# Thirteen steps of the final stream laid beside the last layer's feed-forward

## The chip, the cores and the metric

One core of a Trainium2 chip. The time is that of one execution in device microseconds (us), the median of several runs.

## The reference

A small language-model tower over B = 2 sequences of T = 1024 tokens, all in float32. Two layers (L = 2, width D = 192, 12 heads, feed-forward 768) of banded attention with one global token; each layer ends in

```python
x = layernorm(x + attention(x) @ Wo.T + bo) * g1 + beta1
x = layernorm(x + relu(x @ W1.T + b1) @ W2.T + b2) * g2 + beta2
```

Then a final layernorm and a projection to 128 channels (Wc) give h. A second block takes h through layernorm, a retention scan and a 5-tap depthwise convolution, and a 128-256-128 gelu feed-forward, each with a residual. A last layernorm feeds a router that sends every token to the best of 8 experts (128-512-128, relu); the expert's result, times the router's probability, is added.

## The kernel before

Tokens lie in blocks of P = 128: NB = 8 per sequence, NN = 16 in all. The five engines run their own queues of instructions in program order; semaphores tie them. The work comes in four rounds (2 sequences x 2 layers), then one stream over the 16 blocks, then the experts. All that the change touches is the last round (`rnd == B * L - 1`, sequence 1, layer 1) and the stream.

**The end of a round.** `_seq_c()` (L1696) writes out by hand the order in which every engine walks the feed-forward; `seq_c(rnd)` (L1724) adapts it, and each engine loops over it (POOL L603, ACT L790, DVE L1069, PE L1554) and picks the kinds that it has a part in:
- `y i`, i below 8: attention's output projection of a block. `y i`, 8 to 15: the second feed-forward product of block i - 8, 12 matmul instructions (L1369). Both go to bank i % 4; PE waits with `z_ready` for z i-4. DVE adds the residual (L1084) and takes mean and variance (L922 to L924); POOL raises the variance to the power -0.5 (L545, `rstd`).
- `z i`: DVE normalizes into `zt` (L928); POOL applies gain and bias into `resid` (L551, L552).
- `tr i`: PE transposes `zt` into bank 4 or 5 (L1304, L1305), ACT writes it to `xa`, `xb` (`norm_out`, L699), the input of hid.
- `hid i`, 0 to 11: six products with W1 for each half of the sequence (four blocks), four matmul instructions of 512 columns each into bank 6 or 7 (L1575, L1576); ACT applies relu (L811).

The order is: y 0 to y 7 with z and tr, hid 0 to 2, tr 4, 5, hid 3 to 5, tr 6, 7, then y 8, y 9, z 8, y 10, z 9, y 11, z 10, z 11, hid 6 to 11, and y 12, y 13, z 12, y 14, z 13, y 15, z 14, z 15. In the last round the tr of 8 and above are left out. At y 9 ACT issues two writes of zero rows to the DRAM table `xs` (L804).

**The stream.** `for t in range(NN + DEPTH)`, 29 steps on each engine (POOL L624, ACT L819, DVE L1141, PE L1593). A block passes a stage per step, so step t has block t at the first stage and block t - 12 near the last:
- DVE, step t: adds of blocks t-7 and t-11 from PSUM (L1147, L1152), statistics of four kinds (L1157 to L1175) on block t, t-7, t-11, t-3, the scan of block t-5 (L1185), and, after POOL's power of the step before (L637), the normalizations z0 of block t-1, z1 and x of t-4, z2 of t-8 and the router's row of t-12 (all L1193).
- PE: the convolution of block t-6, ten matmul instructions (L1601), transposes of z0 (L1607, L1608), the scan's product (L1612), the second and first gelu products of t-10 and t-9 (m2 L1619, m1 L1627), the transpose of z1 (L1634), the router's product of t-13 (L1641); then hw, the projection to 128 channels of block t-1 (L1650, L1651), and the transposes of z2 (L1656) and of the router's row (L1661).
- ACT: moves the transposes out of PSUM (L824, L825 into `xa`, `xb`; L837 xn; L842 h0, counted by `kept`; L846; L851) and does gelu (L831). An activation of the 1 x 1 `gs` (L818) ahead of the stream loads Gelu's table.
- POOL: adds (L628, L629, L634) and the power of -0.5 (L637).
In steps 17, 22, 26 and 28 (`CHOSEN`) the router's choice is made for a group of blocks, and POOL scatters rows to `xs` (L619). Experts start when all rows are there.

SP waits for the last y product and then loads the experts' weights. In SBUF the tensors from `h0` on share the space of the attention's; with the declared order only the experts' weights lie ahead of the stream's small buffers.

Of the kernel before, what the change touches and what calls it, by code (L numbers as in the profile page):

```python
# [16 lines left out]
P = 128  # L17
# [10 lines left out]
KC = 5  # L28
# [48 lines left out]
ORDER = (1, 2, 3, 0, 4, 5, 6, 7)  # L77
CHOSEN = tuple(e - 1 + DEPTH for _, e in GROUPS)
# [12 lines left out]
def program(nc, x, xcol, pad, emb, wqkv, wo, w1, w2, lnr, lnl, lnf, wc, ident, band, cols, decay, convw, wout, bo2, owner,  # L91
            ln12, aw1, ab1, aw2, ab2, wg, bg, mwb, mw2, mb2, route, earlier, qrows, krows, out):
    with ExitStack() as ctx:
# [128 lines left out]
        rs = sb("rs", [P, 2, 5], F32)  # L222
        xt = sb("xt", [P, XBUF, RW], F32)
# [191 lines left out]

        def early_step(j, part):

            return -LEAD + PARTS * (j - 3) + part if j >= 3 else None
# [106 lines left out]
        def _(pool):  # L525
# [21 lines left out]

            def residual(b, j):
# [61 lines left out]
            pool.wait_ge(const_in, 16 * len(consts))  # L610
            nc.gpsimd.tensor_tensor(bo2b[:, 0, :], bo2b[:, 0, :], bo2b[:, 1, :], ALU.add).then_inc(bo2_ready, 1)
            pool.wait_ge(bo2_ready, 1)
# [11 lines left out]
            for t in range(NN + DEPTH):  # L624
                i = t - 5
                if 0 <= i < NN:
                    pool.wait_ge(x1_ready, i + 1)
                    nc.gpsimd.tensor_tensor(h0[:, i, :], h0[:, i, :], ab2b[:, :], ALU.add)  # L628
                    nc.gpsimd.tensor_tensor(x1[:, i, :], x1[:, i, :], bo2b[:, 0, :], ALU.add).then_inc(xb_ready, 1)  # L629
                i = t - 8  # L630
                if 0 <= i < NN:
                    pool.wait_ge(xb_ready, i + 1)
                    pool.wait_ge(y_added, i + 1)
                    nc.gpsimd.tensor_tensor(h0[:, i, :], h0[:, i, :], x1[:, i, :], ALU.add).then_inc(xh_ready, 1)  # L634
                if t < NN + DEPTH - 2:
                    pool.wait_ge(stats_ready, t + 1)
                    nc.gpsimd.tensor_tensor(rs[:, t % 2, :], vin[:, t % 2, :], colc[:, 3:4].to_broadcast([P, 5]),  # L637
                                            ALU.pow).then_inc(rs_ready, 1)
# [23 lines left out]
        def _(act):  # L662
# [14 lines left out]
            def first_pieces(j, q):  # L677

                act.wait_ge(qk_mm, at(qk_mm, j + 1, q))
                if j >= 2:  # L680
# [3 lines left out]
                                     ACT.Copy).then_inc(qk_hi, 1)  # L684

# [16 lines left out]
            for b in range(B):  # L702
                for l in range(L):
# [86 lines left out]
                    for kind, i in seq_c(rnd):  # L790
# [15 lines left out]
                        if kind == "hid":  # L806
# [4 lines left out]
                            nc.scalar.activation(hid[:, m, :], ps[6 + i % 2][:, :], ACT.Relu).then_inc(h_relu, 1)  # L811
                            if rnd == 0 and i == FF // P:
# [5 lines left out]
            nc.scalar.activation(gs[0:1, 0, 0:1], lfa[0:1, 0:1], ACT.Gelu)  # L818
            for t in range(NN + DEPTH):  # L819
                i = t - 1  # L820
                if 0 <= i < NN:
                    n = i % NB
                    act.wait_ge(t0_mm, i + 1)
                    nc.scalar.activation(xa[:, blk(n)], ps[0][0:DLO, 0:P], ACT.Identity, bias=lfa[:, 1:2], scale=lfa[:, 0:1])  # L824
                    nc.scalar.activation(xb[0:DHI, blk(n)], ps[0][0:DHI, P:2 * P], ACT.Identity, bias=lfb[0:DHI, 1:2],  # L825
                                         scale=lfb[0:DHI, 0:1]).then_inc(a0_done, 1)
                i = t - 9
                if 0 <= i < NN:
                    act.wait_ge(m1_mm, i + 1)
                    for m in range(2):  # L830
                        ins = nc.scalar.activation(gl[:, i % 2, m, :], ps[7][:, blk(m)], ACT.Gelu, bias=ab1s[:, m:m + 1])  # L831
                    ins.then_inc(gelu_done, 1)
                i = t - 4
                if 0 <= i < NN:
                    b, n = divmod(i, NB)
                    act.wait_ge(t1_mm, i + 1)
                    nc.scalar.activation(xn[:, b, 2 + n * P:2 + (n + 1) * P], ps[1][:, 0:P], ACT.Identity, bias=l12[:, 1:2],  # L837
                                         scale=l12[:, 0:1]).then_inc(a1_done, 1)
                i = t - 1
                if 0 <= i < NN:  # L840
                    act.wait_ge(hw_mm, i + 1)
                    nc.scalar.activation(h0[:, i, :], ps[6][:, 0:DM], ACT.Copy).then_inc(kept, 1)  # L842
                i = t - 8
                if 0 <= i < NN:
                    act.wait_ge(t2_mm, i + 1)
# [975 lines left out]
```

## Time and profile before

| | |
|---|---|
| median of 3 runs | 919.44 us (919.04 to 920.62) |
| profiled execution, its own time | 919.02 us |
| its span, first to last instruction | 916.9 us |
| mean granted TensorE clock | 0.953 |
| PE, DVE, ACT, POOL busy | 809.2, 634.4, 563.3, 567.2 us |
| last feed-forward, hid 0 to the end of y 15 | 715.6 to 754.6 |
| stream, DVE's step 0 to its step 28 | 757 to about 848 |
| experts | about 863 to the end |

The granted clock is given as a share of 2.4 GHz: 1.00 is that, 0.50 is 1.2 GHz. PE is TensorE's matmuls, PEld its weight loads. A timeline's row gives start, length, engine, line, operation, output <- input, count, and in brackets the idle time before it and what ended it.

### The profile page before, as it was taken

The numbers are of one execution on the slowest core, as the hardware profiler recorded it, in microseconds if no ns is written. First come the engines' busy times: TensorE is split into PE (matmuls) and PEld (weight loads), VectorE is DVE, ScalarE is ACT, GpSimd is POOL, SyncE is SP. The second block draws the span as 40 slices with busy tenths as digits, with TensorE's granted clock in tenths as the row PEclk, the third lists the DMA queues.
The fourth block names the chain that finished last, engine by engine and source line by source line (L and its number), as shares of the span: only waits on it lengthen the run. The fifth ranks groups of instructions, "written<-read, shape, count | busy, mean of one in ns | idle before, by whom it ended". The sixth has DMA issues, their size and how long they took to land.

```text
span 916.9 us, 23665 instructions
## 1 busy us (share of the span) xinstructions
PE 809.2 (88%) x8467; PEld 617.3 (67%) x8467; DVE 634.4 (69%) x1959; ACT 563.3 (61%) x1559; POOL 567.2 (62%) x820
## 2 busy tenths in 40 slices
PE   5979998999999989989999899999998986887397
PEld 2757766576777666667776666677766664876397
DVE  2769975547899655578997553689975436988454
ACT  2858885437788853267888543778885423565164
POOL 3638885545388856475888554438885546759345
PEclk8989998999999999999999999999999996997599
DMA  2310000142000012430000024200000245001331
GB/s 65 105 47 3 4 13 11 58 139 77 6 4 3 13 35 87 114 92 26 3 3 14 11 81 116 79 5 4 3 3 2 79 121 205 1 3 41 93 103 39
DMA packets 38595, 43.84 MB, mean 48 GB/s; under 512 B 7162, under 2 KB 33881, under 8 KB 38345
## 3 DMA queue, kind: packets, MB, share of 16 engines
q1 hardware_dynamic: 18348, 19.40, 7.1%
q10 hardware_dynamic: 17860, 18.19, 6.7%
q0 software_dynamic: 2272, 4.74, 1.7%
q8 instruction: 69, 1.13, 0.5%
q14 instruction: 46, 0.38, 0.1%
HBM read 20.70 MB, written 21.59 MB: 46 GB/s over the span
## 4 chain that ended last, share of the span: by engine, by line
PE 59%; DVE 21%; issue 5%; SPq 4%; POOL 4%; ACT 4%; DMA 3%; POOLq 0%; DVEq 0%; ACTq 0%
PE bank L1369 7%; DVE p L1011 6%; DVE nmx L1002 5%; PE bank L1575 5%; PE bank L1457 5%; PE bank L1576 5%; PE bank L1506 4%; PE bank L1530 4%; PE bank L1395 3%; PE bank L1406 3%; PE bank L1460 2%; PE bank L1509 2%; PE bank L1680 2%; PE bank L1601 2%; PE bank L1689 2%
## 5 line engine op out<-in xcount | busy, mean ns | idle before, releaser
L573 POOL TENSOR_TENSOR p<-p 128x384 f16<-128x384 f32 (+1 forms) x320 | 283.8, 907 | 103.4 <-ACT p L746 98.7
L1002 DVE TENSOR_REDUCE nmx<-bank 128x1 f32<-128x384 f32 (+1 forms) x384 | 190.6, 511 | 20.7 <-PE bank L1460 16.2
L744 ACT ACTIVATE p<-bank 128x384 f32<-128x384 f32 (+1 forms) x384 | 170.9, 452 | 54.3 <-PE bank L1509 38.0
L1506 PE MATMUL bank<-stack 103*128 103x128 bf16 x1056 | 145.1, 222 | 5.6 <-DMA stack<-mtr 5.1
L746 ACT ACTIVATE p<-bank 128x384 f16<-128x384 f32 (+1 forms) x320 | 144.3, 451 | 0.0
L1509 PE MATMUL bank<-bandb,idb 128*128 128x128 bf16 x672 | 135.3, 222 | 0.0
L1530 PE MATMUL bank<-vst,p 128*128 128x49 bf16 x2112 | 115.8, 185 | 15.2 <-DVE p L1011 13.6
L1457 PE MATMUL bank<-stack 100*128 100x384 bf16 (+1 forms) x384 | 121.2, 316 | 7.3 <-DVE nmx L1002 2.9
L1530 PEld LDWEIGHTS bank<-vst,p 128*128 128x128 f16 x2112 | 89.5, 97 | 32.4 <-DVE p L1011 19.1
L1506 PEld LDWEIGHTS bank<-stack 103*128 103x128 bf16 x1056 | 88.3, 98 | 29.7 <-issue 14.5
L1460 PE MATMUL bank<-bandb,idb 128*128 128x128 bf16 x672 | 101.2, 220 | 0.0
L545 POOL TENSOR_TENSOR rstd<-ve,colc 128x1 f32<-128x1 f32 x64 | 35.2, 550 | 101.7 <-DVE ve L924 101.7
L1084 DVE TENSOR_TENSOR bank<-bank,resid 128x192 f32<-128x192 f32 x64 | 23.1, 361 | 82.8 <-PE bank L1369 82.8
L1460 PEld LDWEIGHTS bank<-bandb,idb 128*128 128x128 bf16 x672 | 66.0, 98 | 20.9 <-issue 0.8
L811 ACT ACTIVATE hid<-bank 128x512 f32<-128x512 f32 x48 | 28.7, 597 | 81.8 <-PE bank L1576 81.8
L758 ACT ACTIVATE stack<-bank 96x1024 bf16<-96x1024 bf16 x64 | 65.1, 1017 | 18.6 <-PE bank L1395 17.2
L1395 PE MATMUL bank<-idb,hid 128*96 128x128 bf16 x768 | 59.3, 221 | 10.1 <-POOL hid L590 5.2
L1369 PE MATMUL bank<-w2s,hid 128*128 128x192 f32 x384 | 65.1, 328 | 2.8 <-ACT hid L811 2.8
L1369 PEld LDWEIGHTS bank<-w2s,hid 128*128 128x128 f32 x384 | 62.3, 190 | 7.2 <-issue 7.2
L1395 PEld LDWEIGHTS bank<-idb,hid 128*96 128x96 bf16 x768 | 51.2, 124 | 23.4 <-issue 16.8
L1509 PEld LDWEIGHTS bank<-bandb,idb 128*128 128x128 bf16 x672 | 65.6, 98 | 0.7
L1011 DVE TENSOR_TENSOR p<-p 128x384 f16<-128x384 f32 (+1 forms) x64 | 63.2, 987 | 2.2
(253 smaller groups left out, 1818.0 us busy)
## 6 DMA issues: line engine op xcount, KB each, us to landing
xs<-zrow ACTq DMA_DIRECT2D x8, 2193.0 KB, 13.5
xt<-xs SPq DMA_DIRECT2D x23, 129.0 KB, 2.1
w2s<-in_w SPq DMA_DIRECT2D x4, 576.0 KB
mwbs<-in_mwb SPq DMA_DIRECT2D x1, 2064.0 KB, 8.5
mw2s<-in_mw SPq DMA_DIRECT2D x1, 2048.0 KB, 12.8
lnrow<-in_lnr SPq DMA_DIRECT2D x4, 480.0 KB
stack<-mtr SPq DMA_DIRECT2D x96, 3.0 KB
w1b<-in_w SPq DMA_DIRECT2D x4, 291.0 KB
```

The lines of the kernel that those rows point to most:

```text
L573: nc.gpsimd.tensor_tensor(p2[:, u % RING, 0:w], p32[:, u % RING, 0:w], p1[:, u % RING, 0:w], ALU.subtract).then_inc(p2_pool, 1)
L744: ins = nc.scalar.activation(p32[:, s % RING, 0:w], ps[2 + s % 3][:, 0:w], ACT.Exp)
L746: ins = nc.scalar.activation(p1[:, s % RING, 0:w], ps[2 + s % 3][:, 0:w], ACT.Exp)
L1002: nc.vector.tensor_reduce(nmx[:, vn % 3, h:h + 1], nat_bank(v)[:, 0:w], AX.X, ALU.max, negate=True).then_inc(max_done, 1)
L1011: nc.vector.tensor_tensor(p2[:, u % RING, 0:w], p32[:, u % RING, 0:w], p1[:, u % RING, 0:w], ALU.subtract).then_inc(p2_dve, 1)
L1369: ins = mm(y, hid[:, m, blk(n % BPC)], w2s[:, m, :], start=m == 0, stop=m == FF // P - 1)
L1395: ins = nc.tensor.transpose(psb[3 + (3 * b + g) % 2][0:NPIECE, blk(h)], nat[:, b % 2, g * HG + h, :], idb[:, :])
L1457: mm(s_ps[:, 0:len(win) * P], q, stack[0:K_NAT, H + h, blk(win[0], len(win))], start=True, stop=False)
L1460: ins = mm(s_ps[:, blk(i)], idb[:, :], bandb[:, 0 if m < n else 1, :], start=False, stop=(i, m) == edges[-1])
L1506: ins = mm(ps[2 + s % 3][:, blk(i)], stack[0:K_ALL, H + h, blk(m)], stack[0:K_ALL, h, blk(n)], start=True, stop=m == n)
L1509: ins = mm(ps[2 + s % 3][:, blk(i)], idb[:, :], bandb[:, 1 if m < n else 0, :], start=False, stop=True)
L1530: ins = mm(out_ps, pt[:, w % RING, blk(a)], vst[:, m, h, :], start=False, stop=i == HH - 1 and a == len(win) - 1 and pt is p2)
```

## The change

The loop bodies of the stream become functions of t: `stream(t)` on DVE and POOL, `stream_head(t)` and `stream_rest(t)` on PE and ACT. In the last round `seq_c` calls steps 0 to 12 from within the feed-forward; the loops after it start at 13.

```diff
+FILLED = 13
...
+STREAM = {("hid", 1): 1, ("hid", 2): 2, ("hid", 3): 3, ("hid", 4): 4, ("hid", 5): 5, ("hid", 6): 6, ("hid", 7): 7,
+          ("hid", 8): 8, ("hid", 9): 9, ("hid", 10): 10, ("hid", 11): 11}
 def seq_c(rnd):
+    if rnd == B * L - 1:
+        seq = []
+        for kind, i in _seq_c():
+            if kind == "tr" and i >= NB:
+                continue
+            t = STREAM.get((kind, i))
+            if t is not None:
+                seq += [("stat", t), ("head", t), (kind, i), ("rest", t)]
+                continue
+            if (kind, i) == ("hid", 0):
+                seq.append(("stat", 0))
+            if (kind, i) == ("y", 15):
+                seq.append(("stat", 12))
+            seq.append((kind, i))
+            if (kind, i) == ("y", 15):
+                seq += [("head", 12), ("rest", 12)]
+        return seq
```

`stat` is DVE's and POOL's part, `head` and `rest` are PE's and ACT's. On PE `head` holds the convolution, the z0 transposes, scan's product, m2, m1, the z1 transpose and the router's product; `rest` holds hw and the transposes of z2 and of the router's row. On ACT `head` holds the two moves of z0, gelu and xn, `rest` the moves to h0, ht and xm. On every engine a part is issued whole at its place in the order.

The y products of the last round rotate through other banks, so that 0 to 3 are free for the stream:

```diff
+        def y_bank(i, last):
+            return ps[(6 if i >= NB + BPC else 4) + i % 2 if last and i >= NB else i % 4][:, 0:D]
...
             def y_block(i):
                 n = block_of(i)
-                if i >= 4:
-                    pe.wait_ge(z_ready, at(z_ready, i - 3))
-                y = ps[i % 4][:, 0:D]
+                last = rnd == B * L - 1
+                if last and i in (NB, NB + 1):
+                    pe.wait_ge(ln_out, at(ln_out, i - 1))
+                elif i >= 4:
+                    pe.wait_ge(z_ready, at(z_ready, i - 1 if last and i >= NB else i - 3))
+                y = y_bank(i, last)
```

The stream's banks change with it: convolution and scan's product from 4 to 3, m2 from 3 to 5, m1 from 7 to 4, hw from 6 to 2, the router's product from 5 to 6, its ranks from 2 to 7. The first use of each such bank in the stream waits for the z that frees it, for example

```diff
             def stream_head(t):
                 i = t - 6
                 if 0 <= i < NN:
                     b, n = divmod(i, NB)
                     pe.wait_ge(a1_done, min(i + 2, (b + 1) * NB))
                     if i:
                         pe.wait_ge(y_added, i)
+                    else:
+                        pe.wait_ge(z_ready, START[z_ready.num][B * L - 1] + NB)
```

hid still reads `xa` and `xb`, so z0's transposes go to `ata` and `atb`, which the last round no longer needs. The call that loads Gelu's table, and the set-up of DVE and POOL, stand in step 0 of the functions:

```diff
+            def stream_head(t):
+                if t == 0:
+                    nc.scalar.activation(gs[0:1, 0, 0:1], lfa[0:1, 0:1], ACT.Gelu)
                 i = t - 1
                 if 0 <= i < NN:
                     act.wait_ge(t0_mm, i + 1)
-                    nc.scalar.activation(xa[:, blk(n)], ps[0][0:DLO, 0:P], ACT.Identity, bias=lfa[:, 1:2], scale=lfa[:, 0:1])
+                    nc.scalar.activation(ata[:, blk(i % NB)], ps[0][0:DLO, 0:P], ACT.Identity, bias=lfa[:, 1:2],
+                                         scale=lfa[:, 0:1])
...
-            for t in range(NN + DEPTH):
+            for t in range(FILLED, NN + DEPTH):
+                stream_head(t)
+                stream_rest(t)
```

In SBUF the stream's small buffers (`z0` to `rs`) are declared ahead of the experts' weights, so that they lie in space that the attention's `stack` no longer needs.

## Rows read from the trace of the kernel before

**Rows 1.** Busy by stretch: length; PE, PEld, DVE, ACT, POOL; clock; DMA; GB/s.

```profile
735.50:746.50 11.00, 10.28 (x24) 4.16 (x22) 1.98 (x6) 3.65 (x7) 3.81 (x7) 1.00 0.68 193
...
761.00:773.80 12.80, 8.77 (x32) 6.48 (x33) 8.64 (x50) 5.80 (x16) 8.18 (x10) 0.50 0.65 244
773.80:799.20 25.40, 22.43 (x169) 20.22 (x168) 21.28 (x109) 13.75 (x42) 16.61 (x27) 0.94 0.00 1
```

**Rows 2.** Timeline of TensorE, last feed-forward; a bracket holds the idle time before.

```profile
715.62 1.12 PE L1575 MATMUL bank<-xa,w1a 96*128 96x512 f32 x2 [0.24 <-ACT xb L699]
...
727.42 8.04 PE L1369 MATMUL bank<-w2s,hid 128*128 128x192 f32 x48 [0.34 <-ACT hid L811]
...
746.56 8.04 PE L1369 MATMUL bank<-w2s,hid 128*128 128x192 f32 x48 [0.78 <-ACT hid L811]
761.00 0.45 PE L1607 MATMUL bank<-idf,z 128*96 128x128 f32 x1 [6.41 <-DVE z L1193]
```

**Rows 3.** Timeline of DVE, y 9 to z 11 of that feed-forward.

```profile
731.60 0.37 DVE L1084 TENSOR_TENSOR bank<-bank,resid 128x192 f32<-128x192 f32 x1 [0.78 <-PE bank L1369]
...
732.73 0.48 DVE L928 TENSOR_SCALAR zt<-bank,mv,rstd 128x192 f32<-128x192 f32 x1
...
737.43 0.48 DVE L928 TENSOR_SCALAR zt<-bank,mv,rstd 128x192 f32<-128x192 f32 x1 [0.33 <-POOL rstd L545]
```

**Rows 4.** Timeline of POOL: last residuals, and powers of steps 0, 1.

```profile
722.34 0.59 POOL L552 TENSOR_TENSOR resid<-resid,lnrow 128x192 f32<-128x192 f32 x1
...
758.28 0.59 POOL L552 TENSOR_TENSOR resid<-resid,lnrow 128x192 f32<-128x192 f32 x1
...
759.35 2.32 POOL L637 TENSOR_TENSOR rs<-vin,colc 128x5 f32<-128x5 f32 x2
```

**Rows 5.** Timeline of TensorE in step 10, to the start of step 11.

```profile
787.63 1.38 PE L1601 MATMUL bank<-diag,xn 128*128 128x128 f32 x10
788.85 0.27 PE L1607 MATMUL bank<-idf,z 128*96 128x128 f32 x1
...
789.29 0.61 PE L1619 MATMUL bank<-aw2s,gl 128*128 128x128 f32 x4
789.74 0.61 PE L1627 MATMUL bank<-ht,aw1s 128*128 128x128 f32 x4
...
790.29 0.39 PE L1650 MATMUL bank<-wca,xa 96*128 96x128 f32 x2
...
790.74 0.27 PE L1656 MATMUL bank<-idf,z 128*128 128x128 f32 x1
791.41 1.38 PE L1601 MATMUL bank<-diag,xn 128*128 128x128 f32 x10 [0.40 <-ACT xn L837]
```

**Rows 6.** Timeline of DVE: step 6's start and z0; starts of steps 12, 13.

```profile
771.63 0.35 DVE L1157 BATCH_NORM_STATS2 sums<-resid 128x6 f32<-128x192 f32 x1
...
773.54 0.35 DVE L1193 TENSOR_SCALAR z<-resid,mean,rs 128x192 f32<-128x192 f32 x1
...
793.27 0.29 DVE L1147 TENSOR_TENSOR x<-bank,x 128x128 f32<-128x128 f32 x1
...
797.13 0.28 DVE L1147 TENSOR_TENSOR x<-bank,x 128x128 f32<-128x128 f32 x1
```

**Rows 7.** Timeline of ACT: tr 6's first part, and the Gelu table.

```profile
727.17 0.45 ACT L699 ACTIVATE xa<-bank,lna 96x128 f32<-96x128 f32 x1
...
746.43 1.28 ACT L818 ACT_TABLE_LOAD   x1
747.73 0.20 ACT L818 ACTIVATE gs<-lfa 1x1 f32<-1x1 f32 x1
```

**Rows 8.** Busy time by stretch, around a short gap of TensorE.

```profile
576.10:577.70 1.60, 0.01 (x1) 0.02 (x1) 1.53 (x5) 0.85 (x3) 1.60 (x5) 1.00 0.22 47
...
578.60:582.30 3.70, 3.70 (x22) 3.00 (x21) 1.85 (x5) 2.74 (x5) 0.64 (x2) 0.54 0.25 86
```

**Rows 9.** Timeline of POOL, the first scatter.

```profile
826.72 1.09 POOL L619 DMA_INDIRECT xs<-trow,slot  x1
```

More of the change, by code:

```diff
@@ L684, in first_pieces, with stream_rest @@
                                      ACT.Copy).then_inc(qk_hi, 1)
+            def stream_head(t):
+                if t == 0:
+                    nc.scalar.activation(gs[0:1, 0, 0:1], lfa[0:1, 0:1], ACT.Gelu)
+                i = t - 1
+                if 0 <= i < NN:
+                    act.wait_ge(t0_mm, i + 1)
+                    nc.scalar.activation(ata[:, blk(i % NB)], ps[0][0:DLO, 0:P], ACT.Identity, bias=lfa[:, 1:2],
+                                         scale=lfa[:, 0:1])
+                    nc.scalar.activation(atb[0:DHI, blk(i % NB)], ps[0][0:DHI, P:2 * P], ACT.Identity, bias=lfb[0:DHI, 1:2],
+                                         scale=lfb[0:DHI, 0:1]).then_inc(a0_done, 1)
+                i = t - 9
+                if 0 <= i < NN:
+                    act.wait_ge(m1_mm, i + 1)
+                    for m in range(2):
+                        ins = nc.scalar.activation(gl[:, i % 2, m, :], ps[4][:, blk(m)], ACT.Gelu, bias=ab1s[:, m:m + 1])
+                    ins.then_inc(gelu_done, 1)
+                i = t - 4
+                if 0 <= i < NN:
+                    b, n = divmod(i, NB)
+                    act.wait_ge(t1_mm, i + 1)
+                    nc.scalar.activation(xn[:, b, 2 + n * P:2 + (n + 1) * P], ps[1][:, 0:P], ACT.Identity, bias=l12[:, 1:2],
+                                         scale=l12[:, 0:1]).then_inc(a1_done, 1)
+            def stream_rest(t):
+                i = t - 1
+                if 0 <= i < NN:
+                    act.wait_ge(hw_mm, i + 1)
+                    nc.scalar.activation(h0[:, i, :], ps[2][:, 0:DM], ACT.Copy).then_inc(kept, 1)
+                i = t - 8
+                if 0 <= i < NN:
+                    act.wait_ge(t2_mm, i + 1)
+                    nc.scalar.activation(ht[:, i % 2, :], ps[0][:, 0:P], ACT.Identity, bias=l12[:, 3:4],
+                                         scale=l12[:, 2:3]).then_inc(a2_done, 1)
+                i = t - 12
+                if 0 <= i < NN:
+                    act.wait_ge(t3_mm, i + 1)
+                    nc.scalar.activation(xm[:, i % 2, :], ps[1][:, 0:P], ACT.Copy).then_inc(a3_done, 1)
             for k in range(2 * NC):
@@ L811, in _ @@
                             nc.scalar.activation(hid[:, m, :], ps[6 + i % 2][:, :], ACT.Relu).then_inc(h_relu, 1)
+                        if kind == "head":
+                            stream_head(i)
+                        if kind == "rest":
+                            stream_rest(i)
+                        if kind == "hid":
                             if rnd == 0 and i == FF // P:
@@ L1216, in _ @@
+            for t in range(FILLED, NN + DEPTH):
+                stream(t)
                 if t in CHOSEN:
@@ new lines, in stream_rest @@
+            def stream_rest(t):
+                i = t - 1
+                if 0 <= i < NN:
+                    pe.wait_ge(a0_done, i + 1)
+                    if i:
+                        pe.wait_ge(kept, i)
+                    else:
+                        pe.wait_ge(z_ready, START[z_ready.num][B * L - 1] + NB - 1)
+                    mm(ps[2][:, 0:DM], ata[:, blk(i % NB)], wca[:, :], start=True, stop=False)
+                    mm(ps[2][:, 0:DM], atb[0:DHI + 1, blk(i % NB)], wcb[0:DHI + 1, :], start=False, stop=True).then_inc(hw_mm, 1)
+                i = t - 8
+                if 0 <= i < NN:
+                    pe.wait_ge(z2_ready, i + 1)
+                    pe.wait_ge(a0_done, min(t, NN))
+                    nc.tensor.transpose(ps[0][:, 0:P], z2[:, i % 2, :], idf[:, :]).then_inc(t2_mm, 1)
+                i = t - 12
+                if 0 <= i < NN:
+                    pe.wait_ge(z3_ready, i + 1)
+                    pe.wait_ge(a1_done, min(t - 3, NN))
+                    nc.tensor.transpose(ps[1][:, 0:P], trow[:, i, 0:DM], idf[:, :]).then_inc(t3_mm, 1)
@@ L1568, in _ @@
                             ln_transpose(i, i, D)
+                        if kind == "head":
+                            stream_head(i)
+                        if kind == "rest":
+                            stream_rest(i)
                         if kind == "hid":
@@ L1662, in _ @@
+            for t in range(FILLED, NN + DEPTH):
+                stream_head(t)
+                stream_rest(t)
                 if t in CHOSEN:
```

385 lines of the change are left out of this document (175 added, 210 removed).

## The prediction

> **What bounds the kernel now.** I read four views in this order: the busy time by stretch, TensorE's timeline in the last feed-forward, the other engines' timelines beside it, and the clock around a short gap. By stretch [rows 1], TensorE is slow just where the final stream starts: 8.77 of 12.8 us busy at a granted clock of 0.50 (1.2 GHz) in 761.0 to 773.8, behind a gap of 6.41 us [rows 2], then 22.43 of 25.4 us busy up to 799.2. So steps 0 to 5 of the stream leave TensorE room, and steps 6 to 12 nearly none. In the feed-forward it is the other way round: TensorE runs its hid and y products without a pause [rows 2] and DVE is 1.98 us busy in 11 [rows 1]. The change lays the one over the other. What can be gained is the gap and the half rate up to 773.8; what is paid is TensorE work that now stands between the hid products, and waits.
>
> The time is measured from marks in the profiled execution (919.02 us; its span is 916.9 and the rest lies around it; the median of the runs is 0.4 above it). The mark I follow is the start of DVE's step 13, 797.13 us [rows 6], since what follows it is the same in both kernels. Ahead of the mark the stream and the feed-forward take 715.62 to 797.13; I lay out the same stretch for the new order.
>
> **First half, hid 0 to 5 with steps 0 to 5.** hid 0 starts at 715.62 and a hid product takes 1.72 (two pairs of 0.86), so hid 1 stood at 717.34. Now the transposes of step 1 stand ahead of it, in order. They need z0, that needs the power of step 0 on POOL, and POOL first ends the residual of z 7 at 722.34 + 0.59 = 722.93 [rows 4]. In the kernel before the power starts 0.48 after the last residual (758.87 to 759.35), and TensorE's transpose starts 1.65 after that (761.00) [rows 2, 4]. The same spacing gives 725.06: TensorE stands still for 7.7 us. Each of steps 1 to 3 then adds its transposes, 0.22, and the hw product, 0.45 [rows 5] (0.44 stands there for the transposes and the scan's product together, 0.45 for hw); steps 4 and 5 add another transpose, 0.11. Together 3.5. y 8 waits for ACT's second pair of norm_out, which stands behind relu and kept of step 5: two ACTs of 0.45 [rows 7], of which some 0.5 was waited for before too, +0.3.
> The clock: the gap of 7.6 us is longer than the 6.41 us behind which it stood at 0.50 [rows 1, 2]. After a gap of 1.60 us dense work ran on, and of it 3.7 us at a mean clock of 0.54 [rows 8], 1.85 lost; I take 2.0 here, for a clock already down when work resumes. Sum of the half: 7.7 + 3.5 + 0.3 + 2.0 = +13.5.
>
> **The y products.** Before they rotate through four banks; now y 10 waits for z 8, y 11 for z 9, and in the second half y 14 for z 12, y 15 for z 13. On DVE, z 8 is queued behind the adding and the statistics of y 9: 731.60 for y 9's add, 732.73 for z 8, end 733.21 [rows 3]. The y block starts at 727.42 and a product takes 1.95 (8.04 for four, less the tail) [rows 2], so y 10 stood at 731.3 and now starts at 733.3. Then DVE takes y 10's add and statistics ahead of z 9, and y 11 waits 1.9 again. Behind these waits on TensorE stands everything that follows. +3.9 for the four, and +3.9 for y 12 to 15.
>
> **Second half, hid 6 to 11 with steps 6 to 11.** The convolution of step 6 can follow y 11 at once. The transpose of z0 cannot: DVE has z 11 first (it starts at 737.43 and takes 0.48, 2.45 in all from the end of the y products at 735.46 [rows 2, 3]), then step 6 of the stream, whose z0 starts 1.91 into the step and takes 0.35 [rows 6]. TensorE goes on 4.6 after y 11's end, of which 1.2 is convolution. From there it is the bound, and I add its work, each operation by the distance of the starts in step 10 [rows 5]: convolution 1.22 (1.11 to 1.22 in other steps), transposes and scan product 0.44, m2 0.45, m1 and t1 0.55, hw 0.45, t2 0.11, and 1.72 for hid. Step 6 from the transpose on 2.7; step 7 3.9; step 8 4.0; step 9 (with m1) 4.4; steps 10 and 11 (with m2) 4.95 each: 24.9. DVE's step of 3.86 at the most [rows 6] is covered by these, as are ACT's and POOL's parts; if that cover failed, the third rival below comes true. The preload of Gelu's table is called for step 0 of ACT's head alone, and the new order has no such call, so the load (1.28 [rows 7]) falls in step 9, between the transposes and the normalized xn that the next convolution wants; some 2.3 us of hid and hw cover most of the 2.6, +0.3. With 0.1 for the last relu: 4.6 + 24.9 + 0.4 = 29.9 from y 11's end to y 12, against 746.56 - 735.46 = 11.1 before [rows 2]: +18.8.
> The Trainium skill (ScalarE: Activation LUTs, What ACT_TABLE_LOAD costs) gives a drain of about 1.38 us beside the load; the trace has none (the activation starts 1.30 after the load begins), and by the page the sum would be 1.4 higher.
>
> **The end.** y 12 then stands at 746.56 + 13.5 + 3.9 + 18.8 = 782.8, y 15 9.8 later at 792.6. DVE takes step 12 (3.86) ahead of y 15, then y 15's add up to z 15, which like y 11's up to z 11 takes 1.93 and 0.48 (two spacings of 1.95 behind 731.60 the add of y 11 stood at 735.50 [rows 3]): step 13 starts at 792.6 + 6.2 = 798.8, against 797.13. **+1.7**, if the clock falls once only.
> The other drops: TensorE is idle 1.9 ahead of y 10, 1.9 ahead of y 11, 3.4 in step 6, and 1.9 ahead of y 14 and y 15. The row that is nearest is the gap of 1.6 us with 3.7 us at about half rate behind it. No row shows such gaps with bursts of 2 us between them. The bounds for the first group are 0 and 5.8 (y 10 and y 11 wholly at half rate, 1.95 each, and 1.85 at hid 6); I take y 11 and hid 6, 3.8. For the second 0 and 3.9; y 15 at half rate is hidden by DVE's step 12, so part of y 14, 1.0. Below zero neither can go, as the waits are there at either rate. Sum: 1.7 + 3.8 + 1.0 = +6.5, so 919.0 + 6.5, and 0.4 more as median: 925.9.
>
> **Costed at nothing.** The two writes of zero rows, issued at y 9, are over in the stretch up to 746.5 (a DMA share of 0.68 [rows 1]); they move some 17 us later. SP's loads of expert weights wait for the last y product; they are over in the stretch up to 773.8 (0.65 [rows 1]) and move some 40 later. The first scatter that needs the one is at 826.72 [rows 9], and the experts come behind it. The exchange of xa, xb for ata, atb, the other banks and the SBUF order change no duration. POOL's adds and powers of the moved steps fit its idle: 3.81 us busy in 11 at 735.5 to 746.5 [rows 1].
>
> **Rivals.** *The clock holds after the first gap* (y 10 to 15 at full rate): +1.7, 921.1, no measurable change. For it: bursts and hid products are dense once running. Against: the 1.6 us gap [rows 8]. Chance 0.15. The Trainium skill (TensorE: Matmul & The Clock Gate, HAM oscillation) says that a loop whose bursts are shorter than the waits between them pays the slow clock at each; no row here shows that pattern yet.
> *The y products keep their pace*, because z 8, z 9, z 12 and z 13 come in time: this needs each z done within 1.9 us of its own y product, where its place behind the next add puts it 3.8 after. Then 7.8 and the later drops go: 1.7 - 7.8 = -6.1, 913.3, faster. Against it stands the order in DVE's queue, which I can read; but every other gain that I overlook (shorter waits at step 1 or step 6) ends here too. Chance 0.15.
> *Each mixed step waits for a handshake besides its work*, as TensorE waited 0.40 before step 11 for xn [rows 5], now with relu in ACT's queue too: 0.6 in each of 11 steps is 6.6, 932.5. Decides from the point where ACT's or DVE's chain is longer than TensorE's step. Chance 0.17.
> Forecast 0.53.
>
> **Numbers.** A measurement can tell about 0.2%, 1.8 us, from no change. Faster takes the second rival and some of the first: 0.18. Same takes the rest of the first, 0.12, and 0.02 of the forecast's low end: 0.14. Slower 0.68. The range reaches from near the second rival, 914.5, to past the third, 933.5.
>
> **What would show it.** TensorE waits some 7.7 us for z0 ahead of hid 1; y 10, y 11, y 14 and y 15 each start 1.9 us after the product ahead of them has ended; the granted clock falls again in the y block of the first half; the spacing of hid 9, 10, 11 is 4.4 to 5.0 us; DVE's step 13 starts near 803.5. It is wrong if the y products follow each other at 1.95, if the spacing in steps 6 to 11 is over 5.5 us, or if the mark comes ahead of 797.

## The result, and the profile after

The changed kernel takes 923.96 us (median of 6 runs, 919.23 to 926.20), the kernel before 919.24 on the same chip (6 runs, 915.40 to 920.62): a ratio of 1.006, 95% interval 1.0038 to 1.0082. It is slower, by some 4.7 us. The ratios are taken over the single executions, not from the two medians, and of the 25 runs of the kernel before that stand beside e5 to e8 further down, one took 2581.37 us and is left out of the ratios.

| | before | after |
|---|---|---|
| profiled execution, its span | 919.02, 916.9 us | 919.23, 917.0 us |
| mean granted TensorE clock | 0.953 | 0.960 |
| PE, DVE, ACT, POOL busy | 809.2, 634.4, 563.3, 567.2 us | 805.4, 635.3, 561.9, 568.0 us |
| last feed-forward, hid 0 to the end of y 15 | 715.6 to 754.6 | 711.5 to 794.1 |
| DVE's step 13 | 797.13 | 798.02 |

The two profiled executions are equally long though the medians are not. So the first thing to see is where the profiled run of after was ahead. Its hid 0 stands at 711.45 us, that of before at 715.62 [rows 2], in code that is the same up to there. The busy time by stretch of both, over two stretches of that code (length; busy time of PE, PEld, DVE, ACT, POOL with instructions in brackets; granted clock; DMA; GB/s), the kernel before first:

```profile
60.00:70.00 10.00, 8.01 (x80) 6.04 (x80) 5.41 (x12) 6.30 (x23) 5.05 (x9) 0.66 0.01 2
...
570.00:590.00 20.00, 18.00 (x132) 13.49 (x131) 12.49 (x38) 13.73 (x30) 11.26 (x26) 0.91 0.22 60
```

And the kernel after:

```profile
60.00:70.00 10.00, 7.65 (x86) 5.79 (x87) 6.21 (x13) 6.54 (x24) 5.83 (x10) 0.83 0.01 2
...
570.00:590.00 20.00, 18.00 (x153) 13.22 (x152) 14.13 (x40) 15.80 (x33) 10.48 (x25) 1.00 0.30 86
```

Where the clock falls in the earlier rounds differs from run to run; the profiled run of after had the higher clock in both stretches (0.83 for 0.66, 1.00 for 0.91) and is the fastest of its six. Over all that stands ahead of hid 0 TensorE lost 13.0 us to a low clock in it and 15.8 in the run of before (busy time times 1 minus the granted clock, in stretches of 0.5 us): 2.7 of the 4.2 us. The rest was not taken apart. From here on every time is counted from the start of hid 0 of its own run; the stretch from there to DVE's step 22 is nearly all that the kernels differ in.

TensorE at the start of the last feed-forward, kernel after (start, length, line, operation, count, idle time before it and what ended it):

```profile
711.45 1.13 PE L1693 MATMUL bank<-xa,w1a 96*128 96x512 f32 x2 [0.24 <-ACT xb L747]
712.42 1.02 PE L1694 MATMUL bank<-xb,w1b 97*128 97x512 f32 x2
720.89 0.45 PE L1421 MATMUL bank<-idf,z 128*96 128x128 f32 x1 [7.45 <-DVE z L1010]
...
721.34 1.92 PE L1693 MATMUL bank<-xa,w1a 96*128 96x512 f32 x2
```

The gap of 6.41 us that stood at the start of the stream [rows 2] is not gone. It stands ahead of hid 1 and measures 7.45. On DVE step 0's statistics follow z 7, and on POOL step 0's power follows the last residual of z 7 (DVE's first row is step 0, POOL's rows are that residual and the powers of steps 0 and 1):

```profile
717.11 0.36 DVE L974 BATCH_NORM_STATS2 sums<-resid 128x6 f32<-128x192 f32 x1
718.16 0.59 POOL L577 TENSOR_TENSOR resid<-resid,lnrow 128x192 f32<-128x192 f32 x1
...
719.23 2.32 POOL L570 TENSOR_TENSOR rs<-vin,colc 128x5 f32<-128x5 f32 x2
```

The half rate [rows 1] came along, as the stretches show:

```profile
717.50:721.00 3.50, 0.11 (x1) 0.12 (x2) 2.18 (x15) 0.00 (x0) 3.34 (x6) 0.50 0.01 2
721.00:727.50 6.50, 6.50 (x14) 3.62 (x15) 2.53 (x18) 2.47 (x6) 2.07 (x3) 0.50 0.00 0
...
738.50:750.50 12.00, 8.60 (x50) 8.01 (x51) 4.07 (x14) 0.62 (x2) 3.94 (x7) 1.00 1.04 322
750.50:754.50 4.00, 1.10 (x10) 0.91 (x9) 3.48 (x16) 0.00 (x0) 2.57 (x5) 1.00 0.52 157
754.50:758.50 4.00, 3.39 (x8) 2.10 (x9) 3.56 (x17) 1.15 (x3) 3.82 (x7) 0.57 0.00 0
758.50:782.00 23.50, 23.23 (x145) 17.62 (x143) 13.05 (x65) 14.32 (x38) 10.83 (x17) 1.00 0.00 1
782.00:794.00 12.00, 8.53 (x50) 7.97 (x51) 6.23 (x27) 0.44 (x2) 4.75 (x10) 1.00 0.01 1
```

6.50 us of hid products ran wholly at 0.50 (1.2 GHz). The y block takes 12.0 us, 8.6 of them busy, where it was one unbroken row of 8.04 before [rows 2]; the last row but one shows TensorE busy for 23.23 of 23.5 us, the bound that the prediction gave it. The y products themselves and step 6 behind them:

```profile
738.48 4.17 PE L1400 MATMUL bank<-w2s,hid 128*128 128x192 f32 x24 [0.67 <-ACT xb L747]
744.35 2.22 PE L1400 MATMUL bank<-w2s,hid 128*128 128x192 f32 x12 [1.70 <-DVE zt L950]
748.26 2.22 PE L1400 MATMUL bank<-w2s,hid 128*128 128x192 f32 x12 [1.70 <-DVE zt L950]
750.32 1.28 PE L1413 MATMUL bank<-diag,xn 128*128 128x128 f32 x10
755.11 0.45 PE L1421 MATMUL bank<-idf,z 128*96 128x128 f32 x1 [3.51 <-DVE z L1010]
```

y 8 and y 9 run as one row, y 10 and y 11 each wait 1.70 us for a z. (The profile's rows overlap a little: the starts of y 10 and y 11 are 3.91 apart instead of 1.95, so a wait costs 1.96.) DVE's own timeline shows the ring: the add of y 9, z 8 behind it, and only then y 10's add after 2.31 idle:

```profile
742.69 0.37 DVE L1187 TENSOR_TENSOR bank<-bank,resid 128x192 f32<-128x192 f32 x1 [0.78 <-PE bank L1400]
...
743.82 0.48 DVE L950 TENSOR_SCALAR zt<-bank,mv,rstd 128x192 f32<-128x192 f32 x1
746.60 0.37 DVE L1187 TENSOR_TENSOR bank<-bank,resid 128x192 f32<-128x192 f32 x1 [2.31 <-PE bank L1400]
```

In the second half y 14 and y 15 do the same, again TensorE's timeline of after:

```profile
787.91 2.22 PE L1400 MATMUL bank<-w2s,hid 128*128 128x192 f32 x12 [1.70 <-DVE zt L950]
791.83 2.22 PE L1400 MATMUL bank<-w2s,hid 128*128 128x192 f32 x12 [1.70 <-DVE zt L950]
```

And DVE's timeline there: step 12 stands ahead of y 15's add, and step 13 follows at 798.02:

```profile
791.69 0.28 DVE L964 TENSOR_TENSOR x<-bank,x 128x128 f32<-128x128 f32 x1
...
795.62 0.35 DVE L1187 TENSOR_TENSOR bank<-bank,resid 128x192 f32<-128x192 f32 x1
...
798.02 0.28 DVE L964 TENSOR_TENSOR x<-bank,x 128x128 f32<-128x128 f32 x1
```

Where the 5 us come from, by the same marks in both traces (us):

| stretch | before | after | difference |
|---|---|---|---|
| hid 0 to y 8; before with the part of the stream up to step 6, after with steps 0 to 5 inside | 26.38 | 27.03 | +0.65 |
| y 8 to the end of y 11 | 7.88 | 11.84 | +3.96 |
| second half up to y 12, with steps 6 to 11 | 32.90 | 31.76 | -1.14 |
| y 12 to step 13 | 14.36 | 15.94 | +1.58 |
| sum, hid 0 to step 13 | 81.52 | 86.57 | +5.05 |

Laying steps 0 to 11 over the hid products gained half a microsecond in all, with what the low clock costs in either kernel; the two stretches that hold the y products' waits cost 5.5.

### The profile page after: what moved, and what is told of

It reads as the page before. It is cut to its first block, busy times and chain, and to the rows that moved or that the text cites. A ratio compares the mean times of both kernels' runs of the same rounds, so it can differ in the third digit from the quotient of the medians.

```text
span 917.0 us, 23670 instructions
## 1 busy us (share of the span) xinstructions
PE 805.4 (88%) x8467; PEld 614.5 (67%) x8467; DVE 635.3 (69%) x1959; ACT 561.9 (61%) x1558; POOL 568.0 (62%) x820
## 3 DMA queue, kind: packets, MB, share of 16 engines
q8 instruction: 69, 1.13, 0.5%
## 4 chain that ended last, share of the span: by engine, by line
PE 58%; DVE 22%; POOL 5%; issue 5%; SPq 4%; ACT 3%; DMA 2%; POOLq 0%; DVEq 0%; ACTq 0%
PE bank L1400 7%; DVE p L1114 6%; PE bank L1571 5%; DVE nmx L1105 5%; PE bank L1693 5%; PE bank L1694 4%; PE bank L1620 4%; PE bank L1644 4%; PE bank L1509 3%; PE bank L1520 3%; PE bank L1574 2%; PE bank L1623 2%; PE bank L1732 2%; PE bank L1741 2%; SPq L462 2%
```

## The experiments

The table holds every kernel that ran. The marks are us behind the run's own hid 0. "Lost" is TensorE's time lost to a low clock within 104 us of hid 0: busy time times (1 - granted clock), summed over stretches of 0.5 us. The marks and the loss come from one profiled run of each. The ratio is to the kernel before on the same chip; e1 to e4 ran together (before: median 921.84 of 35 runs), e5 to e8 together on another chip (before: 918.91 of 25).

| kernel | y 8 | y 12 | step 13 | step 22 | lost | median us | ratio, 95% interval |
|---|---|---|---|---|---|---|---|
| before | 11.80 | 30.94 | 81.51 | 116.32 | 5.93 | | |
| after | 27.03 | 70.63 | 86.57 | 121.50 | 5.02 | 923.96 | 1.006, 1.0038 to 1.0082 |
| e1_banks | 26.83 | 66.58 | 80.56 | 116.61 | 6.59 | 920.57 | 0.9988, 0.9967 to 1.001 |
| e2_warm | 23.75 | 65.77 | 81.73 | 117.92 | 1.55 | 922.10 | 0.9998, 0.9977 to 1.002 |
| e3_late | 21.15 | 62.30 | 86.77 | 121.91 | 7.84 | 923.52 | 1.003, 1.0005 to 1.0055 |
| e4_second | 12.40 | 47.05 | 82.14 | 116.98 | 3.42 | 920.98 | 0.9988, 0.9964 to 1.0012 |
| e5_second_banks | 12.41 | 43.79 | 77.95 | 112.79 | 5.71 | 913.19 | 0.9951, 0.9929 to 0.9973 |
| e6_banks_warm | 23.76 | 61.46 | 75.44 | 110.73 | 0 | 910.68 | 0.9929, 0.9903 to 0.9956 |
| e7_second_warm | 12.67 | 41.71 | 72.86 | 107.70 | 0 | 908.90 | 0.991, 0.9877 to 0.9942 |
| e8_before_warm | 11.80 | 30.94 | 77.13 | 111.94 | 0 | 912.84 | 0.9952, 0.993 to 0.9973 |

For most kernels the difference at step 22 and the ratio tell the same: +5.2 against 0.6% (5.5 us) for after, -4.4 against -0.48% for e8, -8.6 against -0.9% for e7. They are up to 2.8 us apart for others: +5.6 against 0.3% for e3, +1.6 against nothing for e2. So differences of 1 to 2 us between two kernels at that mark hang on single runs.

**e1_banks: the y products' waits taken away.** The waits hang on the banks that the y products may use, so the experiment gives them others, and moves the waits to where nothing is lost.

```diff
-            return ps[(6 if i >= NB + BPC else 4) + i % 2 if last and i >= NB else i % 4][:, 0:D]
+            return ps[{8: 4, 9: 5, 10: 6, 11: 7, 12: 6, 13: 7, 14: 2, 15: 6}[i] if last and i >= NB else i % 4][:, 0:D]
...
+                elif last and i == 14:
+                    pe.wait_ge(kept, 11)
+                elif last and i == 15:
+                    pe.wait_ge(z_ready, at(z_ready, 13))
                 elif i >= 4:
-                    pe.wait_ge(z_ready, at(z_ready, i - 1 if last and i >= NB else i - 3))
+                    pe.wait_ge(z_ready, at(z_ready, i - 3))
...
+                    if t == 12:
+                        pe.wait_ge(z_ready, START[z_ready.num][B * L - 1] + 15)
...
+                            if rnd == B * L - 1 and i in (6, 7):
+                                pe.wait_ge(z_ready, at(z_ready, i + 5))
```

> The y products of the last round get other banks: y 10 and y 11 take 6 and 7 (hid 6 and hid 7 then wait for z 10, z 11), y 14 takes 2, y 15 takes 6 and waits only for z 12. Nothing else is changed. Theory of the bank waits: TensorE's three waits on the path go, 1.9 us each ahead of y 10, y 11 and y 14 (the one ahead of y 15 is hidden by DVE's step 12), so 5.6 us less than the changed kernel: 924.0 to 918.4. Rival, the waits are hidden by something else (DVE's z 11 and step 6 come at the same time anyway): no change, 924. Rival of the clock: the shorter stretch leaves the drops at steps 1 and 6 as they are, so it adds or takes nothing.

Measured: 0.9988, and 4.9 less than after at step 22. TensorE's timeline of this kernel:

```profile
740.64 8.07 PE L1404 MATMUL bank<-w2s,hid 128*128 128x192 f32 x48 [0.67 <-ACT xb L747]
748.54 1.28 PE L1417 MATMUL bank<-diag,xn 128*128 128x128 f32 x10
753.33 0.33 PE L1425 MATMUL bank<-idf,z 128*96 128x128 f32 x1 [3.52 <-DVE z L1010]
```

The block is one row of 8.07 again. From after's y 8 to its y 12 it saves 3.85, by step 13 6.0; 1.1 of that goes again by step 22, where the clock fell once more (from 84.0 to 87.5 behind hid 0). The waits are real and cost nearly what they seem to (4.9 of the 5.6 expected); without them the change is worth nothing either way.

**e2_warm: the clock held through the waits.** Products of the identity with itself go to a part of a bank that nobody reads, 32 ahead of step 1's transposes and 14 ahead of step 6's. They only keep TensorE busy while it would wait.

```diff
+                    if t == 6:
+                        pe.wait_ge(z_ready, START[z_ready.num][B * L - 1] + 10)
+                    for _ in range({1: 32, 6: 14}.get(t, 0)):
+                        mm(ps[{6: 7}.get(t, 5)][:, 3 * P:4 * P], idf[:, :], idf[:, :], start=True, stop=True)
```

> TensorE does idle products while it waits for z0: 32 of 128 x 128 ahead of step 1's transposes (some 7.1 us) and 14 ahead of step 6's (3.1 us), into banks that nobody reads; their results are used nowhere. Theory of the clock: the profile of the changed kernel shows 6.6 us and 3.3 us of dense work at 0.50 behind the two waits, 5 us lost; with the waits filled the clock stays at 1.00 there and the time falls by some 5 us, 924.0 to 919.0. Rival, the half rate is hidden behind DVE and POOL (the path runs through z0 and the powers): less than 1 us.

Measured: 0.9998. TensorE's timeline of this kernel:

```profile
717.50 7.31 PE L1419 MATMUL bank<-idf 128*128 128x128 f32 x64
725.13 0.32 PE L1425 MATMUL bank<-idf,z 128*96 128x128 f32 x1 [0.33 <-DVE z L1010]
...
725.39 1.02 PE L1697 MATMUL bank<-xa,w1a 96*128 96x512 f32 x2
```

And its busy time by stretch:

```profile
717.50:725.10 7.60, 7.30 (x65) 7.11 (x63) 4.68 (x27) 0.60 (x1) 7.21 (x13) 1.00 0.01 3
725.10:739.40 14.30, 13.50 (x60) 8.09 (x60) 6.95 (x40) 10.37 (x29) 6.53 (x7) 1.00 0.00 0
```

The transposes start 9.46 behind hid 0, as in after (9.44), so the wait is untouched. What changed is the rate: the pair behind them takes 1.02, where it took 1.92 in after. y 8 comes 3.3 earlier, y 12 4.9 earlier: the two low stretches of after, 3.39 and 1.63. At step 22 3.6 are left, because a new low stretch (1.55 lost) came later in the stream, in step 13. TensorE's wait ahead of it, and the stretch:

```profile
800.72 0.45 PE L1425 MATMUL bank<-idf,z 128*96 128x128 f32 x1 [1.55 <-DVE z L1010]
800.40:803.90 3.50, 3.18 (x16) 3.17 (x17) 2.74 (x12) 1.14 (x4) 2.61 (x5) 0.51 1.09 448
```

By the ratio the gain over after is 0.6%, which is what was expected; by the mark it is 3.6 of the 5 us.

**e3_late: the stream begins at hid 2,** when the residual of z 7 is nearly done, so that no long wait stands ahead of a hid product. Steps 1 to 9 then lie beside hid 3 to 11, step 10 behind y 15.

```diff
-FILLED = 13
+FILLED = 11
...
+STREAM = {("hid", 3): 1, ("hid", 4): 2, ("hid", 5): 3, ("hid", 6): 4, ("hid", 7): 5, ("hid", 8): 6, ("hid", 9): 7, ("hid", 10): 8, ("hid", 11): 9}
```

> The steps start two hid products later: step 0 on DVE and POOL at hid 2, steps 1 to 9 beside hid 3 to 11, step 10 at y 15, so steps 11 and 12 go back to the stream behind. Theory of the wait for z0 in step 1: TensorE reaches it with 5.6 instead of 1.8 us of work behind it, waits 3.8 instead of 7.5 us, and two steps' work leaves each half. First half 7.4 us shorter, second half 6.0, end 0.6, stream two steps longer, 7.8: 6 us less than the changed kernel, 918. Rival, steps are worth moving wherever they stand (each saves its 3.9 us of stream): it gets slower than the changed kernel.

Measured: 1.003, no better than after at step 22 (121.91 against 121.50), so the expectation missed. TensorE's wait for z0 in step 1 is 3.58, as expected, but y 8 came only 5.9 earlier (7.4 expected) and y 8 to y 12 is 2.5 shorter (6.0 expected), y 12 so 8.3 earlier in all. Then steps 11 and 12 are back in the stream, and the clock was low three times (3.3, 2.89 and 1.65 lost). The stretches of the second and the third:

```profile
749.20:756.20 7.00, 5.89 (x15) 3.77 (x16) 4.74 (x20) 2.30 (x6) 4.98 (x8) 0.51 0.01 3
...
793.20:797.20 4.00, 3.44 (x17) 3.43 (x18) 2.99 (x15) 1.40 (x5) 2.79 (x5) 0.57 1.10 456
```

Against after, 7.84 - 5.02 = 2.8 us more were lost to the clock, which is up to that much of the missing gain; the rest was not taken apart.

**e4_second: only the second half is filled.** hid 0 to 4 run without a step between them; step 0 stands at hid 5, steps 1 to 6 beside hid 6 to 11, step 7 behind y 15.

```diff
-FILLED = 13
+FILLED = 8
...
+STREAM = {("hid", 6): 1, ("hid", 7): 2, ("hid", 8): 3, ("hid", 9): 4, ("hid", 10): 5, ("hid", 11): 6}
```

> Nothing beside the first half: step 0 on DVE and POOL at hid 5, steps 1 to 6 beside hid 6 to 11, step 7 at y 15, steps 8 to 12 back in the stream behind. Theory: the first half is as in the kernel before (15.2 us shorter than in the changed one), the second half 11.5 shorter, the end 0.9, and the stream 17.0 longer: 10.6 us less than the changed kernel, 913.4, so 6 us faster than the kernel before. Rival, the loss sits in the second half, where TensorE's own work adds up, and the first half pays: then this is no better than the changed kernel.

Measured: 0.9988, 4.5 better than after at step 22 where 10.6 had been expected. y 8 is 0.6 later than before; a wait for z0 (4.44 us) now stands behind y 11, and the clock falls behind it. From y 12 to step 13 it takes 35.09, and there the clock falls a second time; e7, without bank waits and low clock, takes 31.15 for the same. The stretches of e4:

```profile
741.10:745.50 4.40, 0.04 (x1) 0.00 (x0) 3.82 (x15) 0.00 (x0) 2.91 (x6) 1.00 0.69 184
745.50:750.50 5.00, 4.91 (x14) 2.89 (x15) 1.94 (x12) 2.06 (x6) 2.22 (x2) 0.66 0.00 0
...
783.00:788.00 5.00, 4.97 (x29) 4.87 (x29) 3.97 (x22) 2.71 (x6) 3.93 (x8) 0.66 1.04 440
```

What this wait is made of can be read from the same trace. The first row is POOL's power of step 0, the second DVE's z0 from it, the third TensorE's transpose:

```profile
724.56 1.18 POOL L570 TENSOR_TENSOR rs<-vin,colc 128x5 f32<-128x5 f32 x1
744.75 0.78 DVE L1010 TENSOR_SCALAR z<-resid,mean,rs 128x192 f32<-128x192 f32 x1
745.59 0.32 PE L1421 MATMUL bank<-idf,z 128*96 128x128 f32 x1 [4.44 <-DVE z L1010]
```

The power was there at 725.74, 19 us ahead of z0. DVE computes z0 in its step 1, and that stands behind z 11 in its queue: the wait comes of the order alone.

**e5_second_banks** is e4 with e1's banks (y 14 waits for kept 6, step 7's hw for z 15).

```diff
+                elif last and i == 14:
+                    pe.wait_ge(kept, 6)
...
+                    if t == 7:
+                        pe.wait_ge(z_ready, START[z_ready.num][B * L - 1] + 15)
```

> Steps 1 to 6 beside the second half alone, as in e4_second, with the y banks of e1_banks. Theory of the bank waits: as in e1_banks the waits ahead of y 10, y 11 and y 14 go, 5.6 us less than e4_second, so about 0.994 of its ratio: 0.993 of the kernel before, 913. By marks: DVE's add of step 22, 117.0 us behind hid 0 in e4_second, at 111.4. Rival of the clock: with the waits gone TensorE is no longer idle there, and a drop goes too, up to 2 us more. Rival, the waits were hidden in this order: no change against e4_second.

Measured: 0.9951, 4.2 less than e4 at step 22. The banks are worth about the same in both places, 4.9 on after and 4.2 on e4. The expectation had 5.6 and, in the rival of the clock, one low stretch less; more was lost to the clock instead, 5.71 against 3.42 in e4, as 6.59 against 5.02 in e1. If that was all on the path, the banks gave 6.5 us in both places, an estimate from these four losses and marks.

**e6_banks_warm** is e1 with idle products ahead of steps 1, 6, 12 and 13, and Gelu's table loaded at step 0, early, as the kernel before had it.

```diff
+                        if kind == "stat" and i == 0:
+                            nc.scalar.activation(gs[0:1, 0, 0:1], lfa[0:1, 0:1], ACT.Gelu)
...
+                    if t in {6: 10, 12: 14}:
+                        pe.wait_ge(z_ready, START[z_ready.num][B * L - 1] + {6: 10, 12: 14}[t])
+                    for _ in range({1: 32, 6: 14, 12: 6, 13: 8}.get(t, 0)):
+                        mm(ps[{1: 5, 6: 5, 12: 7, 13: 7}[t]][:, 3 * P:4 * P], idf[:, :], idf[:, :], start=True, stop=True)
```

> All thirteen steps moved, y banks of e1_banks, Gelu's table loaded at step 0 again, and idle products in TensorE's waits: 32 ahead of step 1, 14 ahead of step 6, 6 ahead of step 12's and 8 ahead of step 13's transposes (results used nowhere). The trace of e1_banks has three stretches at 0.50 ahead of step 22, with 6.6 us lost, and step 9 pays 0.4 for the table. Theory, bank waits and clock explain the loss and add up: the add of step 22, 116.6 behind hid 0 in e1_banks, comes at 110, and the time is 0.992 of the kernel before, 912 to 914. Rival, the half rate is hidden behind DVE and POOL: 116.

Measured: 0.9929. At step 22 it is 10.8 ahead of after; e1 and e2 alone were 4.9 and 3.6 ahead. It is the whole change, all 13 steps where the change puts them, with both costs taken out.

**e7_second_warm** is e5 with the same treatment: 18 idle products ahead of step 1, 4 and 8 ahead of steps 7 and 8.

```diff
+                    if t in {1: 10, 7: 14}:
+                        pe.wait_ge(z_ready, START[z_ready.num][B * L - 1] + {1: 10, 7: 14}[t])
+                    for _ in range({1: 18, 7: 4, 8: 8}.get(t, 0)):
+                        mm(ps[{1: 5, 7: 7, 8: 7}[t]][:, 3 * P:4 * P], idf[:, :], idf[:, :], start=True, stop=True)
```

> As e5_second_banks, with Gelu's table loaded at step 0 and idle products ahead of the transposes of step 1 (18), 7 (4) and 8 (8). Theory of the clock: the two stretches at 0.50 of e4_second (1.7 us each) go: 3.4 less than e5_second_banks, the add of step 22 at 108, 0.989 of the kernel before. If it equals e5_second_banks, the clock was not on the path. Against e6_banks_warm it tells whether the first half is worth anything once waits and clock are out: equal says that steps 1 to 5 cost in the first half what they cost in the stream.

Measured: 0.991, 908.9 us, the fastest of all. TensorE's timeline ahead of and at step 1's transposes:

```profile
738.32 4.20 PE L1425 MATMUL bank<-idf 128*128 128x128 f32 x36
742.93 0.31 PE L1431 MATMUL bank<-idf,z 128*96 128x128 f32 x1 [0.41 <-DVE z L1012]
```

And its busy time by stretch from there on, at a clock of 1.00 throughout:

```profile
742.90:759.40 16.50, 16.19 (x75) 10.22 (x75) 9.44 (x52) 9.96 (x27) 9.02 (x10) 1.00 0.07 20
759.40:771.80 12.40, 11.01 (x71) 10.38 (x72) 8.42 (x33) 1.23 (x4) 6.51 (x11) 1.00 0.22 63
771.80:790.60 18.80, 16.82 (x137) 15.48 (x138) 17.28 (x84) 9.17 (x28) 15.11 (x25) 1.00 0.56 211
```

**e8_before_warm** is the kernel before with nothing moved: 28 idle products ahead of step 1's transposes, 3 ahead of each hw of steps 1 to 5.

```diff
+                    for _ in range(28 if t == 1 else 0):
+                        mm(ps[7][:, 3 * P:4 * P], idf[:, :], idf[:, :], start=True, stop=True)
                     pe.wait_ge(z0_ready, i + 1)
...
+                    for _ in range(3 if t <= 5 else 0):
+                        mm(ps[7][:, 3 * P:4 * P], idf[:, :], idf[:, :], start=True, stop=True)
                     pe.wait_ge(a0_done, i + 1)
```

> The kernel before, with nothing moved: 28 idle products ahead of step 1's transposes and 3 ahead of each hw of steps 1 to 5, so that TensorE stays busy in the gap ahead of the stream. The trace before has 17 us at 0.50 there, about 5.9 us of TensorE's time. Theory, half rate on TensorE's chain is what the move saves: the add of step 22 comes 3 to 5 us earlier than 116.3, and the time is 0.995 to 0.997 of the kernel before, with nothing moved. Rival, DVE, ACT and POOL set the pace of steps 0 to 6 whatever the clock: no change.

Measured: 0.9952. The same stretches as in [rows 1], laid 0.8 earlier, as its hid 0 stands at 714.79:

```profile
760.18:773.00 12.82, 10.97 (x81) 9.40 (x82) 10.48 (x59) 7.09 (x20) 9.42 (x12) 1.00 0.64 242
773.00:798.40 25.40, 22.60 (x185) 20.62 (x184) 23.67 (x122) 15.30 (x47) 18.07 (x29) 1.00 0.00 1
```

In [rows 1] the first read 0.50. The clock stays whole and step 13 comes 4.4 earlier; y 8, y 12 and the distance from step 13 to step 22 (34.81) are what they were. The gap stays, filled with idle products; what its half rate costs could be had for less than the change: 4.4 us of the 5.93 lost, with no step moved.

## Why the prediction was right, and where its terms were off

The sign and the range held: forecast 925.9, measured 923.96; by the marks +5.05 where +6.5 was forecast. Term by term, counted from hid 0:

| term | forecast | measured |
|---|---|---|
| idle ahead of hid 1 | 7.7 | 7.45 |
| steps' work in the first half, with y 8's wait | 3.8 | 4.4 (15.23 - 7.45 - 3.39) |
| half rate behind the first wait | 2.0 | 3.39 |
| y 10 and y 11 | 3.9 | 3.96 |
| end of y 11 to y 12, without the clock (forecast from the end of y 11's row, measured from the start of what follows, 0.16 earlier) | 29.9 | 30.13 (31.76 - 1.63) |
| clock behind y 10's wait | 3.8 | 1.63 |
| y 12 to y 15 | 9.8 | 9.75 |
| clock behind y 14's and y 15's waits | 1.0 | 0 |
| y 15 to step 13 | 6.2 | 6.19 |

**What was read from queues held to 0.3 us.** That z 8 stands behind y 9's add on DVE, that step 12 stands ahead of y 15's add, that z0 of step 6 comes behind z 11: each gave its wait (3.96 for 3.9, 6.19 for 6.2, and 7.45 for 7.7 ahead of hid 1). The work of the steps in the first half was put 0.6 too low. e1 confirms by experiment what the y waits are worth: without them the changed kernel is no slower than before. The rival in which the y products keep their pace was rejected for the right reason.

**The step that failed is the clock.** The forecast took 2.0 for the first stretch, "for a clock already down when work resumes", from a stretch [rows 8] behind a gap of 1.60; the nearer row was the gap of 6.41 with 0.50 behind it [rows 1, 2], and what followed 7.45 us was 6.50 us of dense work at half rate. In the other direction it took 4.8 for falls behind y 10 and behind y 14. The clock read 1.00 through both y blocks (738.5 to 750.5, 782.0 to 794.0), waits included, and fell once more, behind the idle 3.51 us of step 6. The three errors, +1.4, -2.2 and -1.0, make -1.8; the other terms bring back 0.4 (from the same starting point the row of 29.9 is off by 0.1 only), and -1.4 is what lies between forecast and marks. That the errors partly cancel is luck. The first rival had said that the clock holds through the y blocks, and was right about that; its 921.1 left out the fall at step 6 and had the first one at 2.0 too. On the oscillation that the Trainium skill describes (TensorE: Matmul & The Clock Gate, HAM oscillation), for bursts shorter than the waits between them, this trace does not decide: the bursts here are 2.22 us and the waits 1.70.

**The third rival,** a handshake in each mixed step, did not come: hid 8 to 11 start 3.83, 4.40, 5.22 and 4.84 us apart, 4.4 to 5.0 had been forecast for the last three, and TensorE is 99% busy there. The 5.22 holds Gelu's table, in step 9 as forecast, since the order never calls step 0 of ACT's head:

```profile
769.59 1.28 ACT L710 ACT_TABLE_LOAD   x1
770.88 0.37 ACT L710 ACTIVATE gl<-bank,ab1s 128x128 f32<-128x128 f32 x1
```

The activation starts 1.29 after the load; the extra drain that the Trainium skill gives (ScalarE: Activation LUTs, What ACT_TABLE_LOAD costs) is not seen here either, so the sum without it was the better one.

**Why the change doesn't pay.** The gap of 6.41 and the half rate were what could be gained. The profile after shows that in the order that the change gives them they were not on offer in the first half. z0 waits for the power of step 0. The power stands in POOL's queue behind the last residual of z 7, which ends 7.3 us behind hid 0 (718.16 + 0.59 - 711.45), and the statistics of step 0 stand behind z 7 on DVE. Taking steps 0 to 5 to hid 1 to 5 puts the wait of the stream's start ahead of hid 1 instead.

That wait is one of order in the queues and not of data. Block 0 of the stream is the first block of sequence 0, whose residual POOL wrote two rounds earlier. In the trace of after it ends at 365.46, 350 us ahead of step 0's statistics, and DVE waits for `resid_ready` with the count of that round:

```profile
364.87 0.59 POOL L577 TENSOR_TENSOR resid<-resid,lnrow 128x192 f32<-128x192 f32 x1
```

The `stack`, in whose space the change puts the stream's small buffers, is read for the last time at 699.4, 12 us ahead of hid 0. POOL is idle for 2.76 us up to 704.38, and a power takes 1.2. The bank that the transposes of step 1 go to is free with z 5, which ends at 713.48, just as hid 0 does (713.44) and 7.4 us ahead of where they start. So the nearest rival of this change is the same thirteen steps with step 0's statistics and power, and z0, some places earlier on DVE and POOL. It is in no run: what it would gain, and what it would delay on either engine, is not shown.

For the order as it is, e6 and e7 measure what the first half is worth: both without bank waits and without low clock, they differ in where steps 0 to 12 stand (and in the idle products, 60 and 30), and e7, which leaves the first half alone, is 3.0 ahead at step 22. Against e8, where nothing is moved and the clock is whole too, e7 is 4.2 ahead and e6 1.2. So at full rate and without bank waits the steps beside the second half, with the other banks, gain 4.2, and the move into the first half gives back 3.0 of it. The runs agree in the order of the three (medians 908.90, 910.68 and 912.84), but the intervals of their ratios overlap, so the sizes rest on one trace of each. The change as made pays the y waits (4.9) on top, and keeps nearly all the clock loss that the kernel before had (5.02 against 5.93).

Still open: what an earlier step 0 is worth, how e6's and e7's early Gelu table and their last idle products divide what these two gained over e1 and e5, and what e3 lost beside the clock.

## What to carry to other kernels

A wait moves with the work that it stands in. Before laying a chain over other work, look up two things for its first input: when the data are ready, and which instructions stand ahead of the one that makes it in its engine's queue. If the data are late, start the chain no earlier. If only the place in the queue is late, as here and in e4, that instruction is the one to move first; no run here has tried it. When a bank rotation is shortened from four to two, each product waits for the reader of the one before the last, at its place in the reader's queue; here that cost could be read from the timeline before the change to a tenth of a microsecond. And where a wait leaves TensorE idle for several microseconds ahead of dense work, products that nobody reads can hold its clock: that took 0.5% off the kernel before with not one step moved, and 0.9% with the steps beside the second half only and the other banks (908.9 us, faster than both kernels).

## What the runs showed beyond that

- An idle product of the identity takes 0.23 us in two passes (32 in 7.31 us), and needs an input that is there anyway. It delays nothing as long as the block ends ahead of the awaited event; e2 left 0.33 us.
- The clock read 1.00 through four waits of 1.70 us with bursts of 2.22 between them, and 0.50 to 0.66 behind waits of 3.51 (after), 4.44 (e4) and 7.45 us (after). e1 had the 3.5 us wait too, and 0.57 for 4 us behind it. A long wait isn't needed: in the stream it fell in e2 at 84.7 behind hid 0, in e5 at 57.1 and in e4 at 67.3, where the longest idle time in the 9 us before was 1.55, 1.32 and 1.13 us. What tells these from the four waits of 1.70 was not taken apart.
- Where the clock falls differs from run to run. The kernel before ran from 912.3 to 920.3 beside e5 to e8 (24 runs without the one of 2581.37); e6, e7 and e8, whose profiled runs keep the clock whole for 104 us behind hid 0, from 909.1 to 912.6, from 908.0 to 911.9 and from 910.0 to 915.8 (8, 6 and 12 runs). That the spread is smaller because of the clock is not shown. One profiled run against one other would have called the change a tie; the marks behind hid 0 told it from a single trace of each.
